# Windowed attention: one value slot instead of two in the key product, the values placed by VectorE, and a projection with two forms of weights

## The reference, cut to what matters

```python
xn  = layernorm(x over channels) * g + b
xs  = roll(xn, (-3, -3));  xw = windows of 7x7 tokens          # N = 49 tokens, 256 windows an image
q, k, v = split(xw @ qkv_w + qkv_b)                            # 3 heads of 16 channels
attn = softmax(q @ k.T * 16 ** -0.5 + rel_bias)                # 49x49 for each head and window
out = (attn @ v) @ proj_w + proj_b
x   = x + roll back(out)
x   = x + fc2(gelu(fc1(layernorm(x over channels))))           # 48 -> 192 -> 48
```

## Time and profile before

| | |
|---|---|
| median of 3 runs | 1970.64 us (1966.45 to 1970.95) |
| the profiled execution | 1975.34 us, its span 1973.7 us |
| busy: PE, ScalarE, VectorE, POOL | 1772.9 us (90%), 1541.7 us (78%), 1365.0 us (69%), 1170.0 us (59%) |
| copies of the values (L725) | 256 on ScalarE, 488 ns each |
| granted TensorE clock, mean | 0.951 of full speed |

### The profile page before, as it was taken

The page is one execution under the profiler, slowest core; times in us unless marked ns, Lnnn a source line. Parts: engine busy times, 40 slices in busy tenths (PEclk is TensorE's granted clock), DMA queues, the critical chain, the costliest instruction groups (busy, mean ns, idle before and its releaser), DMA issues. The chain is left out here.

```text
span 1973.7 us, 90330 instructions
## 1 busy us (share of the span) xinstructions
PE 1772.9 (90%) x38186; PEld 1076.4 (55%) x38186; DVE 1365.0 (69%) x2016; ACT 1541.7 (78%) x2904; POOL 1170.0 (59%) x1048
## 2 busy tenths in 40 slices
PE   4999999999999999999999998995899967999996
PEld 2666556656565565655666565651497943333332
DVE  7776666767676676766767676642777766888883
ACT  3788788888888788888888888873766647888882
POOL 5687686777778677777877777652255550122222
PEclk9999999999999899999999999996799985999998
DMA  4344554444444344444444444411488759999994
GB/s 111 94 108 99 139 129 103 105 102 110 100 113 102 96 107 100 116 99 105 106 107 103 104 112 99 98 45 43 109 216 216 214 135 170 227 253 253 262 258 147
DMA packets 233228, 262.26 MB, mean 133 GB/s; under 512 B 167079, under 2 KB 179911, under 8 KB 232711
## 3 DMA queue, kind: packets, MB, share of 16 engines
q1 hardware_dynamic: 217478, 217.50, 46.2%
q0 software_dynamic: 15360, 39.08, 6.6%
HBM read 160.82 MB, written 80.88 MB: 122 GB/s over the span
## 5 line engine op out<-in xcount | busy, mean ns | idle before, releaser
L416 POOL TENSOR_TENSOR shift<-const_b,qmax 113x588 bf16<-113x588 bf16 x256 | 299.4, 1170 | 231.8 <-DVE qmax L511 230.1
L563 DVE TENSOR_TENSOR x<-ps_m,x 112x392 f32<-112x392 f32 x128 | 66.5, 561 | 272.8 <-PE ps_m L1028 272.8
L511 DVE TENSOR_REDUCE qmax<-ps_s 113x12 f32<-113x588 f32 x256 | 194.9, 761 | 66.8 <-PE ps_s L907 66.7
L1487 POOL DMA_DIRECT2D out_rolled<-r_OUT x128 | 63.8, 503 | 270.2 <-DVE r_OUT L1587 270.2
L716 ACT ACTIVATE P<-ps_t 113x588 f32<-113x588 f32 x256 | 172.0, 672 | 58.4 <-PE ps_t L959 57.1
L748 ACT ACTIVATE G<-ps_m 128x392 f32<-128x392 f32 x384 | 178.3, 500 | 46.0 <-PE ps_m L1009 45.5
L503 DVE TENSOR_TENSOR Ul<-Uf 113x784 bf16<-113x784 f32 x192 | 208.5, 1113 | 0.0
L1333 PE MATMUL conv_ps<-xin,band_now 64*64 64x448 bf16 x2688 | 203.1, 364 | 2.2 <-DVE x_low L1228 2.2
L406 POOL TENSOR_TENSOR xhl<-xh 113x784 bf16<-113x784 f32 x64 | 200.7, 3137 | 2.2 <-DVE xh L551 2.2
L709 ACT COPY Uf<-ps_m 113x392 f32<-113x392 f32 x384 | 172.9, 486 | 33.0 <-PE ps_m L874 24.8
L1333 PE MATMUL conv_ps<-x_low,band_now 64*64 64x448 bf16 x1344 | 179.6, 351 | 0.0
(11 more groups left out here) (244 smaller groups left out, 5203.9 us busy)
## 6 DMA issues: line engine op xcount, KB each, us to landing
xin<-rows_scratch SPq DMA_DIRECT2D x96, 236.0 KB, 3.8
XT<-x_tokens SPq DMA_DIRECT2D x64, 294.0 KB, 3.3
X<-x_windows SPq DMA_DIRECT2D x128, 147.0 KB, 3.4
RS<-rs_scratch SPq DMA_DIRECT2D x128, 147.0 KB, 3.4
XR<-x_windows SPq DMA_DIRECT2D x128, 147.0 KB, 3.2
x_scratch<-x SPq DMA_DIRECT2D x128, 147.0 KB, 3.4
y_scratch<-y POOLq DMA_DIRECT2D x96, 196.0 KB, 2.9
r_RS<-rs_scratch SPq DMA_DIRECT2D x128, 147.0 KB, 4.6
```

The lines of the kernel that those rows point to most:

```text
L416: nc.gpsimd.tensor_tensor(shift[:, j % 2], e, m, ALU.mult).then_inc(S["md"], 1)
L511: nc.vector.tensor_reduce(qmax[:, j % 2, :].rearrange("p (b n) -> p b n", b=2), ps_s[0:R, :, 0:2 * HQ].rearrange("p b (n t) -> p b n t", t ...
```

## The change

`Uf` and `Ul` get one value slot instead of two (`UV = HEADS + 1`), filled with plain value weights, so the key product has 196 columns for each window instead of 245, with as many products. In the diff, the added `keep_values` is VectorE's, and the removed calls of it, one for each quad, are ScalarE's. The zeros that keep the two groups apart are no longer computed: `V` is cleared once, at the start, and each group's values are copied into its own columns, which are every second column (`V[..., p]`). The groups lie on different partitions, so it takes two copies a quad. These are done by VectorE instead of ScalarE. Since the exponential and the copies read the same banks of `ps_t`, they are put in an order: for quads 0 and 1 the copies wait for the exponential, for quads 2 and 3 the exponential waits for the copies. In the second half of a strip the two groups' columns come out exchanged, so the order of windows is exchanged there too (`b ^ j // 2`), `O` is laid out by kind `a`, and the projection has a form of its weights for each kind. It still takes one product for each of two banks, with 392 columns; `first_residual` reads and writes in pieces of 98 columns.

```diff
-        UV = HEADS + 2
+        UV = HEADS + 1
...
-        V = sb("V", [R, 2, QP, 2 * C])
+        V = sb("V", [R, 2, QP, C, 2])
...
-        O = sb("O", [2 * C, 2, STRIP])
+        O = sb("O", [2 * C, 2, 2, QUADS, 2 * TOK])
...
+        def kept_values(p, j):
+
+            lo = ROWB * p
+            to = V[lo:lo + TOK, j % 2, :, :, p].rearrange("p (b k) c -> p b k c", b=2)
+            of = ps_t[lo:lo + TOK, :, 0:2 * SV].rearrange("p b (k c) -> p b k c", c=SV)[:, :, :, HQ:HQ + C]
+            return to, of
...
-            for t in (wv, wv_swap, blank, margin, x2):
+            for t in (wv, V, blank, margin, x2):
...
+            def keep_values(s, j):
+
+                if s.real:
+                    q = 4 * s.n + j
+                    wait(dve, S["st"], q + 1)
+                    if j < QUADS // 2:
+                        wait(dve, S["ex"], q + 1)
+                    wait(dve, S["pv"], q - 1)
+                    for p in range(2):
+                        nc.vector.tensor_copy(*kept_values(p, j)).then_inc(S["vev"], 1)
...
                 divide(prv, 2)
                 query_max(s, 2)
+                keep_values(s, 0)
                 token_sums(s.at(4))
                 token_squares(s.at(3))
                 divide(prv, 3)
                 normalise0(nx2)
                 query_max(s, 3)
+                keep_values(s, 1)
                 first_residual(prv)
                 normalise1(old)
                 divide(s, 0)
+                keep_values(s, 2)
                 u_low(nxt, 0)
                 u_low(nxt, 1)
                 subtract_mean(prv)
                 u_low(nxt, 2)
                 query_max(nxt, 0)
                 divide(s, 1)
+                keep_values(s, 3)
                 query_max(nxt, 1)
...
             def exp_scores(s, j):
                 if s.real:
                     q = 4 * s.n + j
                     wait(act, S["st"], q + 1)
+                    if j >= QUADS // 2:
+                        wait(act, S["vev"], 2 * (q + 1))
                     wait(act, S["pv"], q - 1)
...
-                keep_values(s, 0)
...
-                    w = QP * j + 2 * b + k
+                    w = QP * j + 2 * (b ^ j // 2) + k
...
-                        mm(bank("proj", b)[0:R, 0:HALF], proj_w[:], O[:, s.slot(2), cols_of(b)],
+                        mm(bank("proj", a)[0:R, 0:HALF], proj_w[:, a, :], O[:, s.slot(2), a],
```

More of the change, by code:

```diff
@@ L521, in divide @@
                     wait(dve, S["proj"], 2 * (s.n - 1))
-                    nc.vector.tensor_tensor(O[:, s.slot(2), W * j:W * j + W], ps_out, rden[:, j % 2, :], ALU.mult
+                    nc.vector.tensor_tensor(O[:, s.slot(2), :, j, :], halves(ps_out), halves(rden[:, j % 2, :]), ALU.mult
                                             ).then_inc(S["nrm"], 1)
@@ L530, in first_residual @@
                     wait(dve, S["x2_made"], 2 * (s.n - 1))
-                    for b in range(2):
-                        wait(dve, S["proj"], 2 * s.n + b + 1)
+                    for a in range(2):
+                        wait(dve, S["proj"], 2 * s.n + a + 1)
                         nc.vector.scalar_tensor_tensor(
-                            out=x1[:, r, cols_of(b)], in0=bank("proj", b)[0:R, 0:HALF], scalar=out_b[:, 0:1],
-                            in1=XR[:, r, cols_of(b)], op0=ALU.add, op1=ALU.add).then_inc(S["x1_made"], 1)
+                            out=of_kind(x1[:, r, :], a), in0=bank("proj", a)[0:R, 0:HALF].rearrange("p (j t) -> p j t", j=QUADS),
+                            scalar=out_b[:, 0:1], in1=of_kind(XR[:, r, :], a), op0=ALU.add, op1=ALU.add
+                            ).then_inc(S["x1_made"], 1)
             def subtract_mean(s):
@@ L634, in _ @@
                 lo = ROWB * g
[L635 to L638 removed]
+                link(nc.vector.tensor_copy(wv[lo:lo + C + 1, 0:C], ps_s[lo:lo + C + 1, 1, 0:C]))
             assert chain[0] == WV_V
@@ L783, in step @@
                 gelu(old, 1, 0)
-                keep_values(s, 3)
                 gelu(old, 1, 1)
@@ L797, in _ @@
             for r in range(2):
[L798 to L803 removed]
+                nc.scalar.copy(Uf[:, r, HEADS, :].rearrange("p (w t) -> p w t", t=TOK),
+                               wv[:].unsqueeze(1).to_broadcast([R, WINS, TOK])).then_inc(values_spread, 1)
             steps(step, -1, N + 2)
@@ L922, in keys_and_values @@
                     wait(pe, S["ex"], q)
-                    wait(pe, S["vev"], q)
+                    wait(pe, S["vev"], 2 * q)
                     r = s.slot(2)
@@ L1794, in constants @@
         ones[lo:lo + TOK, lo:lo + TOK] = 1
-        for b in range(2):
-            key_ones[lo:lo + TOK, b, DH * (g ^ b):DH * (g ^ b) + DH] = 1
+        key_ones[lo:lo + TOK, :, g] = 1
     out["picks"] = np.concatenate([pick, ones, minus], 1)
-    out["key_ones"] = key_ones.reshape(R, 4 * DH)
+    out["key_ones"] = key_ones.reshape(R, 2 * DH)
     out["eye"] = np.eye(128, dtype=f)
@@ L1859, in packs_of @@
         put(a, PACK_A, "w2_part", prm0["fc2_w"][F1:HID], F2 * g)
-        for h in range(HEADS):
-            put(a, PACK_A, "proj_w", prm0["proj_w"][DH * h:DH * h + DH], 2 * DH * h + DH * g, lo)
+        for kind in range(2):
+            first = PACK_A["proj_w"].start + R * kind + ROWB * (g ^ kind)
+            a[g:2 * C:2, first:first + C] = prm0["proj_w"]
         put(a, PACK_A, "bias", by_query, lo)
```

57 lines of the change are left out of this document (20 added, 37 removed).

## The result

The changed kernel takes 2285.87 us (median of 4 runs, 2280.50 to 2286.32) where the kernel before took 1968.55 on the same chip (1965.45 to 1970.95): a ratio of 1.161, 95% interval 1.159 to 1.164. It is slower by 317 us, twice the forecast's 155, and above its range (2035 to 2143). The profiled execution has a span of 2278.8 and took 2280.5.

The account below looks back on a forecast made before the run. A ring through VectorE, POOL, TensorE and gelus, 20.09 us a step, was taken as the bound; 61 x 2.61 - 4 = +155 on 1975.34 gives 2130, or 2126 as median (0.58); range 2035 to 2143.

Parts of the forecast that it names:

- The bound: A closed chain across VectorE, POOL, TensorE and the gelus sets the 20.09 us step; key product and ScalarE's copies lie off it.
- the ring: Chain from second residual through first residual, low1, fc1, gelu and fc2 to the next second residual: 20.09 us, no slack.
- A pair of copies at 0.76: VectorE's two copies a quad, to the next instruction's start, with both changes of partition group costing: 0.76 us; 0.56 without.
- rival 2: VectorE's partition changes cost nothing, pairs take 0.56: 2101 us if POOL goes first (0.09), 2015 if VectorE does (0.05).
- The first residual at 7.13: VectorE's first residual starts 7.13 us behind the second instead of 6.06: +1.52 for two pairs, +0.05, -0.32, -0.18.
- -0.18 for the reduce ahead of the quotient: On VectorE ahead of the first residual, t_var hands over 0.08 early and the quotient's wait for rden goes: -0.18 us.
- `t_mean` gave its 0.32: On VectorE ahead of the first residual, t_mean comes after POOL's shift instead of beside it: -0.32 us.
- Who gets the interface: POOL's low1 asks 0.48 us ahead of VectorE's low parts and wins: low1 takes 1.49, the two low parts 3.94.
- Rival 1: VectorE gets the SBUF interface before POOL's low1: +1.39 us a step, 2051 us; chance 0.17.
- `fc1` at 15.41: TensorE's fc1(old, 0) starts at 15.41 us of the step instead of 12.80, 4.95 behind low1's start: +2.61 a step.
- Behind `fc1` nothing gets shorter: From the start of fc1(old, 0) through gelus and fc2 to the next second residual: 7.29 us, taken as unchanged.
- The setup's -4: In the setup, POOL's spreading of the value weights (8.01 us) halves: -4 us once.

Follow-up runs that it names:

- the copies on ScalarE: Changed kernel with the two copies of each quad given back to ScalarE, all other edits kept: 1975.50 us, ratio 1.003 to the kernel before.
- six products: Changed kernel with six products of constants (218 columns each) ahead of fc1(old, 0), computing nothing that is used: 2142.58 us, ratio 1.092 to the kernel before.
- centring later: Changed kernel with POOL's token centring (t_cen) moved two places later, behind the next shift and squares_low: 2160.47 us, ratio 1.097 to the kernel before.
- four products: Changed kernel with four products of constants (218 columns each) ahead of fc1(old, 0): 2170.34 us, ratio 1.103 to the kernel before.
- five: Changed kernel with five products of constants (218 columns each) ahead of fc1(old, 0): 2152.41 us, ratio 1.096 to the kernel before.
- 224 products of the scores' kind: Changed kernel with quad 0's query-bias and query-score products done nine times instead of once ahead of fc1(old, 0): 2554.35 us, ratio 1.297 to the kernel before.
- seven long products: Changed kernel with seven products of constants (218 columns each) ahead of fc1(old, 0): 2183.15 us, ratio 1.106 to the kernel before.
- two pairs: Changed kernel with the copies of quads 0 and 1 back on ScalarE, those of quads 2 and 3 on VectorE: 2186.86 us, ratio 1.108 to the kernel before.

## Why the prediction was wrong, step by step

- **The bound**: right. Lengthening the ring through the first residual, `low1` and `fc1` lengthened the step, and the key product was worth nothing, though it got shorter as forecast: its six batches take 787.88 - 787.32 = 0.56, 0.12 less than before.
- **A pair of copies at 0.76**: right. It takes 0.74, and 0.77 to the next start. Both changes of partition group cost on these copies what the setup's rows showed; at 0.56, rival 2 is out.
- **The first residual at 7.13**: 7.22. The wait of the first pair for the exponential costs 0.08 and not 0.05: the exponential ends 1.89 behind the second residual (forecast: 1.90), and the first copy starts 0.09 behind that end, here as in the 19 other steps that were read in the middle.

```profile
763.97 0.66 ACT L740 ACTIVATE P<-ps_t 113x588 f32<-113x588 f32 x1 [2.59 <-PE ps_t L966]
```

Of the -0.18 for the reduce ahead of the quotient only 0.06 came: 767.35 - 766.47 = 0.88 instead of 0.94. `t_mean` gave its 0.32. The wait of 0.1 for the projection went, but it stood ahead of the first half of the residual; the two halves still take 1.16.

- **Who gets the interface**: right. POOL asks 0.54 ahead (forecast 0.48), `low1` takes 1.49 and the low parts 3.78. Rival 1 is out.
- **`fc1` at 15.41**: 15.71, +2.91 a step instead of +2.61. `low1` comes 3.42 behind the first residual as before, where I had taken 0.1 off, and F 5.07 behind it instead of 4.95.
- **"Behind `fc1` nothing gets shorter", a rest of 7.29**: this step failed, the one that I took as given. It asked whether anything gets shorter, and not whether anything gets longer. The rest is 9.20 in the median and about 10.6 in the longer steps, since the clock is at 0.50 for most of it. The strip of 228.01, from which the 4.95 was taken, had shown it in the trace of the kernel before: behind TensorE's 1.28 of idle time the clock is at 0.50, and the next second residual comes at 237.55. The windows:

```profile
225.00:230.00 5.00, 3.22 (x83) 2.09 (x82) 5.00 (x7) 3.40 (x7) 1.58 (x2) 0.94 0.60 171
230.00:235.00 5.00, 4.91 (x78) 2.55 (x76) 0.93 (x2) 4.16 (x9) 5.00 (x4) 0.50 0.31 76
```

and VectorE's timeline:

```profile
237.55 1.04 DVE L563 TENSOR_TENSOR x<-ps_m,x 112x392 f32<-112x392 f32 x2 [5.47 <-PE ps_m L1028]
```

Its rest is 237.55 - 228.01 = 9.54. I took the 4.95 from this strip and the 7.29 from the normal one. Both from this strip would have given, by my estimate, 15.41 + 9.54 = 24.95 a step (measured: 24.91) and 1970.64 + 61 x 4.86 - 4 = 2263 us.

- **The setup's -4**: about right. The spreading takes 2.95 now, 5.06 less than the earlier trace rows, and with the copies on ScalarE the first of the 60 steps starts 3.5 earlier (88.6 instead of 92.1).

The sum, over the 60 steps. With six products, which keep the clock in 59 of them and don't move F, they take 1384.5 us: 1384.5 - 1223.8 = 161 is what the longer ring costs (the forecast's terms give 60 x 2.61 = 157). The remaining 1525.7 - 1384.5 = 141 come with the halved clock. That 161 is less than 60 x 2.90 (22.99 - 20.09) = 174 comes from the kernel before having some longer steps of its own (mean 20.40); so it is in part luck that the forecast's 157 is so near, since F was 0.3 a step short. In time, the run with six products is 178 above its kernel before, some 17 more than its steps show; about 13 of these lie outside the 60 steps of the profiled execution: 4.8 ahead of them (the first starts at 96.9 instead of 92.1) and the rest behind them, which I haven't followed.

The step of the prediction that failed is thus the term of 7.29 behind `fc1`: 141 of the 302 us by which the steps grew. All cases of the range varied who waits for whom, and none had a slower engine.

## What to carry to other kernels

Where an edit makes TensorE wait once more in every turn of a ring, price two things: the wait, and the work of TensorE behind it at the lower clock; here the second was nearly as large as the first. A cheap way to tell them apart is a few long products of constants in the idle stretch: if the time falls and the clock stays up, it was the clock. Where a row is taken from an odd strip, read that strip to its end. And before an operation moves to VectorE, look at what it moves against POOL's work on the shared interface: the two low parts took 1.85 before, 3.15 with the copies on ScalarE, 3.45 with the pairs of quads 2 and 3 on VectorE and 3.78 with all four.

## What was unexpected of the hardware

- Idle stretches of 2.15 and 2.35 us on a TensorE that is otherwise busy were followed by a clock of 0.50 for most of the next 7 us, in nearly every step. In the kernel before no such stretch stands in the normal step, and the clock over 60 to 1300 us is 0.99. Shorter ones were less sure: with 1.22 in the median (centring later) the clock was lower behind `fc1` in 44 of 60 steps, with 0.32 (copies on ScalarE) in 4, in the kernel before in 5. With four products in the stretch 18 of 60 steps still had a longer rest, with five 8, with six one.
- 224 products of the scores' kind in a row weren't issued without a break: pauses of 1.00 and 3.03 us lay within them. In the run with seven long products the scores' own 24 had one of 0.94 in the step read, with TensorE waiting for nothing that the profile shows.
- POOL won the interface to SBUF when it asked 0.54 us ahead of VectorE (and 0.88 ahead with two pairs); with VectorE 0.09 ahead `low1` took 2.23 us in the median and the low parts 3.15. With POOL 0.06 ahead VectorE did both low parts first. What decides it I don't know.
